# VectorE's duties planned gap by gap between the evictions of a shared PSUM bank

## The reference

```python
x = x + attn(layernorm(x))
x = x + ffn(layernorm(x))
# attn
q, k, v = split(h @ qkv_w.T)                    # 16 heads of 16
q_weights = exp(|q - centers|^2 * inv_var)      # 16 splats per head; k_weights alike
logits = einsum('bihs,bjhs,hs->bijh', q_weights, k_weights, amplitudes) / temp
out = softmax(logits, over j) @ v, then @ out_w.T
# ffn
xr, xk = mu * h + (1 - mu) * h_prev             # h_prev: the token before
out = sigmoid(xr @ W_r.T) * (relu(xk @ W_k.T)**2 @ W_v.T)
```

## Time and profile before

| | |
|---|---|
| median of 3 runs | 2163.5 us (2162.55 to 2164.25) |
| the profiled execution | 2162.01 us |
| its span, first to last instruction | 2160.2 us |
| mean granted TensorE clock | 0.998 |
| instructions | 52461 |

### The profile page before, as it was taken

One profiled execution on the slowest core, in us unless ns is written; L12 is line 12 of the kernel. 1 busy time (PEld: TensorE's weight loads), 2 busy tenths in 40 slices (PEclk: granted clock), 3 DMA queues, 4 the chain that ended last, 5 costly groups with the idle time before them and its releaser, 6 DMA issues.

```text
span 2160.2 us, 52461 instructions
## 1 busy us (share of the span) xinstructions
PE 2129.8 (99%) x22996; PEld 975.8 (45%) x22996; DVE 742.1 (34%) x1684; ACT 2013.2 (93%) x2190; POOL 386.5 (18%) x486
## 2 busy tenths in 40 slices
PE   7999999999999999999999999999999999999999
PEld 5444444444444444444444444444444444444445
DVE  5324433233432432433323334324323223323225
ACT  3899999999999999999999999999999999999995
POOL 0244243333100142022101203320310000000000
PEclk9999999999999999999999999999999999999999
DMA  6554445353221334316131332523252141311111
GB/s 179 141 147 121 123 125 147 107 154 112 67 68 51 94 109 109 97 41 174 27 91 28 112 94 72 138 60 99 61 144 53 41 90 41 61 30 48 33 41 44
DMA packets 176232, 193.06 MB, mean 89 GB/s; under 512 B 88529, under 2 KB 108369, under 8 KB 175985
## 3 DMA queue, kind: packets, MB, share of 16 engines
q1 hardware_dynamic: 166720, 174.69, 29.3%
q0 software_dynamic: 7168, 14.69, 2.7%
q10 hardware_dynamic: 2096, 0.14, 0.1%
HBM read 98.90 MB, written 75.81 MB: 81 GB/s over the span
## 4 chain that ended last, share of the span: by engine, by line
PE 90%; ACT 7%; DVE 2%; issue 1%; DMA 0%; DVEq 0%
PE ps_pv L889 40%; PE ps_scores L870 27%; PE ps_step L917 17%; ACT probs L1214 6%; PE ps_step L938 2%; PE ps_scores L902 1%; PE ps_step L896 1%; PE ps_scores L907 1%; ACT weight L1278 0%; PE ps_scores L912 0%; PE ps_scores L911 0%; DMA x_prep<-x 0%; DVE weight L1478 0%; DVE ffn_stats L1381 0%; DVE h_ffn L1395 0%
## 5 line engine op out<-in xcount | busy, mean ns | idle before, releaser
L1214 ACT ACTIVATE probs<-ps_scores 128x1024 f32<-128x1024 f32 x2048 | 1941.1, 1030 | 82.7 <-PE ps_scores L870 56.4
L889 PE MATMUL ps_pv<-probs,vals 128*32 128x512 f32 (+5 forms) x10104 | 1079.8, 520 | 0.0
L870 PE MATMUL ps_scores<-q_aug,k_aug 49*128 49x512 f32 x4096 | 706.2, 442 | 8.1 <-ACT probs L1214 5.9
L870 PEld LDWEIGHTS ps_scores<-q_aug,k_aug 49*128 49x128 f32 x4096 | 331.2, 184 | 617.2 <-ACT probs L1214 563.6
L889 PEld LDWEIGHTS ps_pv<-probs,vals 128*32 128x32 f32 x10104 | 349.4, 139 | 201.1 <-issue 118.2
L1336 POOL DMA_DIRECT2D packed<-qk x224 | 113.5, 512 | 871.9 <-DVE qk L1501 850.2
L1341 POOL TENSOR_TENSOR packed<-qk 32x512 f32<-32x512 f32 x224 | 238.2, 1064 | 16.9
L1346 POOL TENSOR_TENSOR k_act<-k_act 128x512 f32<-128x512 f32 x28 | 29.5, 1054 | 817.8 <-DVE k_act L1504 817.8
L1567 DVE COPY o_raw<-ps_pv 128x512 f32<-128x512 f32 x63 | 43.6, 691 | 247.3 <-PE ps_pv L889 246.6
L1501 DVE COPY qk<-ps_step 128x512 f32<-128x512 f32 x56 | 38.7, 690 | 223.9 <-PE ps_step L917 223.9
L1478 DVE TENSOR_SCALAR weight<-ps_step,cen_sq 128x512 f32<-128x512 f32 x57 | 42.8, 750 | 198.0 <-PE ps_step L938 197.1
(11 more groups left out here) (207 smaller groups left out, 1126.6 us busy)
## 6 DMA issues: line engine op xcount, KB each, us to landing
k_aug<-k_parts SPq DMA_DIRECT2D x128, 192.0 KB, 5.0
q_aug<-q_parts SPq DMA_DIRECT2D x128, 192.0 KB
k_parts<-parts SPq DMA_DIRECT2D x32, 512.0 KB, 3.3
q_parts<-parts SPq DMA_DIRECT2D x32, 512.0 KB, 4.7
packed<-qk POOLq DMA_DIRECT2D x224, 64.0 KB, 2.2
x_ffn<-x SPq DMA_DIRECT2D x18, 512.0 KB, 4.8
k_parts<-parts SPq DMA_DIRECT2D x32, 256.0 KB, 4.0
q_parts<-parts SPq DMA_DIRECT2D x32, 256.0 KB, 5.3
```

The lines of the kernel that those rows point to most:

```text
L870: mm = pe.matmul(ps_scores[:, g % RING, e, :], k_aug[rows, s % 2, pair, kt * P:(kt + 1) * P], q_aug[rows, u % 2, pair, :], start=True, sto ...
L889: mm = pe.matmul(ps_pv[32 * c:32 * c + 32, at], vals[:, s % 2, kt, :, c], probs[:, tick % PROB_SLOTS, c, at], start=(kt == 0), stop=(kt == ...
L1214: act.activation(probs[:, tick % PROB_SLOTS, 2 * pair:2 * pair + 2, :], ps_scores[:, g % RING, :, :], ACT.Exp).then_inc(probs_ready, 1)
```

## The change

The places of the duties are no longer fixed ticks but come from a planner, `pace_duties`. Each duty has an earliest tick (the one it had before, for most), a due tick, a tick by which it is needed at a reduction of maxima, and a price (a gap has 12). The planner goes through the gaps in order. In a gap it adds up the prices of the evictions and the take, and then puts in the ready duty with the earliest due tick, as long as the sum stays within the gaps up to the next one (`GAP_WORK * (gap + 2)`); a duty whose due tick is passed or is at most one tick ahead goes in regardless. Within a tick the order is now spread, invert, scaling, ffn layernorm, mix, done, norm, statistics, split.

`norm_tick` moves from 5 to 9 ticks ahead of k0, and with it the earliest ticks of statistics and norm, and SP's ticks for the store and the load of the norm rows. `x_tick` gives the same ticks as before. TensorE's, ScalarE's and GpSimd's programs stay as they are, and so do VectorE's evictions and takes.

The core of the diff:

```diff
 def norm_tick(task):
-    return max(begin(task, "k0") - 5, 1)
+    return max(begin(task, "k0") - 9, 1)
...
+DUTIES = {
+    "spread": [(KT * (u + 1) + 1, KT * (u + 1) + 3, KT * (u + 1) + 4, 3, u) for u in range(UNITS - 1)],
+    "invert": [(KT * (u + 1) + 2, KT * (u + 1) + 4, KT * (u + 1) + 4, 4, u) for u in range(UNITS - 1)],
+    "scale": [(KT * (u + 1) + 3, KT * (u + 1) + 5, KT * (u + 1) + 4, 3, u) for u in range(UNITS - 1)],
+    "ffn_ln": [(tick, begun(task, "turn0") - 4 + part, begun(task, "turn0"), (8, 5, 5, 6)[part], (task, part))
+               for tick, found in FFN_LN_AT.items() for task, part in found],
...
+    "stats": [(tick, tick + 3, norm_tick(task) - 8, (8, 5, 6)[part], (task, part)) for tick, found in STATS_AT.items() for task, part in found],
...
+}
+GAP_WORK = 12
+URGENT = 1
+EVICT_WORK = 3
+OVER = 1
...
+def pace_duties():
...
+    for gap in range(2 * EVENT_TICKS // 3):
+        tick, end_of_next = name_of(gap), GAP_WORK * (gap + 2)
+        now = max(now, GAP_WORK * (gap + 1)) + EVICT_WORK * ((tick in evicts) + (gap in takes))
+        held = name_of(gap + 1) in evicts
+        until = name_of(gap + 1) if name_of(gap + 1) in MAX_AT else 0
+        while True:
+            forced = [duty for duty in waiting if duty[2] <= until and duty[0] < until]
+            ready = forced or [duty for duty in waiting if duty[0] <= tick + 1 - gap % 2]
+            if not ready:
+                break
+            duty = min(ready, key=lambda duty: (duty[1], duty[0], duty[3]))
+            _, due, _, kind, which, work = duty
+            if not forced and due > tick + URGENT and now + (work - OVER if held else 0) > end_of_next:
+                break
+            paced[DUTY_ORDER[kind]].setdefault(tick, []).append(which)
...
-                for u in LEAVE_AT.get(tick, ()):
+                for u in DUTY_AT["spread"].get(tick, ()):
                     spread(u)
```

More of the change, by code:

```diff
@@ L391, with begun @@
 DONE_AT = beside((end(task, "v1") + 1, task) for task in FFNS if task != LAST_BUT)
+def begun(task, name):
+    return begin(task, name) if (task, name) in SPAN else EVENT_TICKS
+DUTIES = {
[4 more added lines that the diff above has]
+               for tick, found in FFN_LN_AT.items() for task, part in found],
+    "mix": [(tick, begun(task, "r0") - 2 + part if part < 2 else begun(task, "k0") - 4 + part,
+             begun(task, "r0") if part < 2 else begun(task, "k0"), 5, (task, part))
+            for tick, found in MIX_AT.items() for task, part in found],
+    "done": [(tick, tick + 6, tick + 1, 5, task) for tick, found in DONE_AT.items() for task in found],
+    "norm": [(tick, begun(task, "k0") - 2 + half, norm_tick(task) + 2, 6, (task, half)) for tick, found in NORM_AT.items() for task, half in found],
+    "stats": [(tick, tick + 3, norm_tick(task) - 8, (8, 5, 6)[part], (task, part)) for tick, found in STATS_AT.items() for task, part in found],
+    "split": [(tick, tick + 3 - side, split_tick(task, half, 1) + 2, (5, 6)[side], (task, half, side)) for tick, found in SPLIT_AT.items() for task, half, side in found],
+}
@@ new lines, with gap_of_values @@
+DUTY_ORDER = list(DUTIES)
+GAP_WORK = 12
+URGENT = 1
+EVICT_WORK = 3
+OVER = 1
+def gap_of_values(tick):
+    return 2 * ((tick + 2) // 3) + int(tick % 3 == 0)
+def pace_duties():
+    waiting = sorted((tick, due, need, DUTY_ORDER.index(kind), which, work) for kind, found in DUTIES.items()
+                     for tick, due, need, work, which in found)
+    evicts = {tick for tick, found in EVICT_AT.items() if any(task[0] != "ffn" or name not in ("r0", "r1") for task, name in found)}
+    takes = {gap_of_values(KT * (u + 1) - 1) for u in range(UNITS - 1)}
+    paced = {kind: {} for kind in DUTY_ORDER}
+    now = 0
+    for gap in range(2 * EVENT_TICKS // 3):
[13 more added lines that the diff above has]
+            paced[DUTY_ORDER[kind]].setdefault(tick, []).append(which)
+            now += work
+            waiting.remove(duty)
+    assert not waiting, waiting[:3]
+    return paced
@@ L394, in load @@
+DUTY_AT = pace_duties()
 def load(gap):
@@ L1688, in _ @@
                     take(tick // KT)
-                for u in LEAVE_AT.get(tick, ()):
+                for u in DUTY_AT["spread"].get(tick, ()):
                     spread(u)
-                for u in LEAVE_AT.get(tick - 1, ()):
+                for u in DUTY_AT["invert"].get(tick, ()):
                     invert(u)
@@ L1694, in _ @@
                     replicate(u, slice(0, CHUNK)).then_inc(den_inverted, 1)
-                for u in LEAVE_AT.get(tick - LEFT_TICKS + 1, ()):
+                for u in DUTY_AT["scale"].get(tick, ()):
                     v.wait_ge(den_inverted, INVERT_STEPS * (u + 1))
                     v.tensor_tensor(o_raw[:, u % 2, :], o_raw[:, u % 2, :], den_all[:, :], ALU.mult).then_inc(scaled, 1)
[L1698 to L1708, removed]
+                for task, part in DUTY_AT["ffn_ln"].get(tick, ()):
                     n = FFN_NO[task]
@@ L1712, in _ @@
                     layernorm("ffn", n, x_ffn[:, n % 2, :, :], h_ffn, ffn_ln, part)
-                for task, half, side in SPLIT_AT.get(tick, ()):
+                for task, part in DUTY_AT["mix"].get(tick, ()):
+                    mix(task, part)
+                for task in DUTY_AT["done"].get(tick, ()):
+                    n = FFN_NO[task]
+                    v.wait_ge(step_free, STEP_NO[task, "v1"] + 1)
+                    finish(n, slice(0, TT)).then_inc(finished, 1)
+                for task, half in DUTY_AT["norm"].get(tick, ()):
+                    normed_columns(task, half)
+                for task, part in DUTY_AT["stats"].get(tick, ()):
+                    statistics(task, part)
+                for task, half, side in DUTY_AT["split"].get(tick, ()):
                     late_split(task, half, side)
```

## The result

| kernel | median us (lowest to highest, runs) | profiled execution: time, span |
|---|---|---|
| before | 2162.65 (2161.99 to 2164.25, 20) | 2162.01, 2160.2 |
| after | 2165.77 (2163.22 to 2168.42, 20) | 2167.36, 2165.5 |

The ratio is 1.0014, with a 95% interval from 1.0007 to 1.0020: slower by 0.14%, which lies inside the 0.2% that was called no change ahead. The forecast, 2169.8, was 4.0 us too high. Of these, 0.9 are the median of before, which these 20 runs put at 2162.65; the other 3.2 are the change, which was forecast at +6.3 and is +3.1. The kernel after also varies more, over 5.2 us where the kernel before varies over 2.3.

The account below looks back on a forecast made before the run. TensorE and ScalarE were taken as each other's bound, VectorE able to give back under 15.6 us. Terms +3.3, +3.4 and -0.4 made +6.3 us on the 2163.5 median: 2169.8, range 2163 to 2174.5.

Parts of the forecast that it names:

- Place one: At (prep 1,1) statistics wait for x, delaying dist_k0: 4.6 us, clock 1.7, less 3.0 at k1; net +3.3 (-0.8 to +6.6).
- Place two: At turn0 of (ffn 0,3), (1,0), (2,0), (3,1), the layernorm's part 3 comes later: +3.4 us in sum.
- the forecast's other side: At the four turn0, ScalarE might hold 0.4 us at each, leaving 1.8 us of the 3.4.
- The clock's price for the first of the four: At turn0 of (ffn 0,3), if TensorE's clock falls at 916 us, 1.7 us on top, making the four 5.1.
- Small gains: At turn0, dist_k1 and v1, evictions no longer late: -0.4 us for the three together, bounds 0 and 1.2.
- All else: Other duties, SP's other waits and norm rows shift slightly; slack covers them, so no cost.
- The forecast's own case: Whole kernel slower by +4.3 to +9 us, around +6.3; chance 0.60.
- losses absorbed: Rival: SP, clock or ScalarE's ring hides part; +1.5 to +2.3 us, within 0.2%, 2165 us; chance 0.25.
- The planner doing what it says: Rival: faster by 4.7 us, 2158.8, if x lands before 216.0 us, so is issued by 209.6; chance 0.06.
- GpSimd's work lengthening a duty: Rival: duties behind q or k evictions run 0.8 us longer; five add 4 us, 2174 us; chance 0.06.
- three signs of being wrong: x lands by 216 us, ScalarE shows no idle stretch behind the waits, or new late evictions stand elsewhere.
- these eleven: Eleven evictions start over 0.2 us late behind the attention bank's take at the same tick boundary; said to stay.

Follow-up runs that it names:

- the layernorm edit: Kernel after, with the due ticks of the four ffn layernorm parts three ticks earlier: 2160.13 us, ratio 0.9990 to before.
- eviction ahead of take: Kernel after with x loaded 30 ticks ahead, layernorm parts due three ticks earlier, and at twelve ticks VectorE's product copy put before the take: 2154.13 us.
- both edits: Kernel after with loads of x 30 instead of 24 ticks ahead of k0 and layernorm parts due three ticks earlier: 2158.17 us, ratio 0.9978 to before.
- the scaling earlier: Kernel after with the scaling of unit 3 one tick earlier, ahead of the first query take's eviction: 2163.53 us, ratio 1.0002 to before.
- the second with the old constant: Kernel after with norm_tick back to 5 ticks ahead of k0, planner kept, run and traced a second time: 2163.24 us.
- x earlier: Kernel after with loads of x and its columns 30 instead of 24 ticks ahead of k0: 2163.45 us, ratio 1.0003 to before.

## Why the prediction came out as it did

**Place one: the mechanism was right in each link, the size was nearer to that of the two traces with the late landing.** Issue of x "near 216" was 215.2 to 216.1, dist_q0's load was forecast to be free at 225.0 and was at 225.01 in the profiled execution, its wait forecast at 4.6 was 4.42. The step that was off is that x "lands 6.4 us later", taken from one row. In the four traces it is 5.3 twice and 7.2 or 7.3 twice, and with 5.3 the net of place one is 1.61 + 0.14 - 3.35 = -1.6, a small gain, against +1.9 with 7.3 and +3.3 forecast. The bounds given, -0.8 to +6.6, hold +1.9 and miss -1.6. The forecast looked for its lower bound in SP being in time, and not in a load that lands early.

**The terms of place one.** Where the clock falls, the loss is 5.26 us against the 6.3 of the forecast. Its parts can be told by setting the traces with 2.43 us of waiting and a full clock beside those with 4.42 and half: the former cost 1.75, so of a wait the usual 0.27 and 0.4 more don't count (that ScalarE's ring holds the 0.4 is argued, not shown); the clock is 1.5 where 1.7 was forecast. 4.42 - 0.27 - 0.4 + 1.5 = 5.25. The forecast had left out both subtractions (0.4 as a bound at turn0 alone), and at k1 it took 3.0 where 3.36 came back. Together that is 1.4 us of the 3.2 between forecast and measured change. If the early landings, worth 3.5 us, come in about half of the executions, as in two of four traces, they make the other 1.8; this is an estimate from four traces.

**Place two was right:** 3.4 forecast, 3.76 measured at once and 3.4 for good, each of the four within 0.12 us. At first ScalarE hides none of it, one for one as argued from the row at 919.50; three exponentials later it has back 0.14, 0.14 and 0.08 us of three of them, where the forecast's other side allowed 0.4 at each. The clock's price for the first of the four, kept as a bound, is paid in some executions and not in others.

**Small gains** were -0.4 and are -0.34. **"All else" at nothing** held: no further step over 0.3 us, except the early stretch at half clock, which lasts 3.41 us in three of the thirteen traces (before, the layernorm edit, and eviction ahead of take) and 6.83 in the ten others. The kernel before was traced once, so whether the change has a part in that is open. In the profiled execution it cost 0.8 us, a term that the forecast doesn't have.

**The rivals.** The forecast's own case, +4.3 to +9 with a chance of 0.60, did not come true by its time, though the time lies inside the range. The case that did is the one given 0.25, losses absorbed (within 0.2%), with its size of +1.5 to +2.3 just under the measured +3.1. By its reasons it is half true: at place one a load that lands early hides part, at turn0 0.36 us of 3.76 come back and the rest counts. The planner doing what it says is what both edits together show, 4.7 us under before, the size worked out for it. Its condition was put too hard, though: x issued at 212.81, not by 209.6, was enough for place one to cost nothing, since a wait that ends before dist_q0 wants the bank at 220.4 is free, and the statistics need not end before dist_k0 is ready. Of GpSimd's work lengthening a duty there is no step in the account, and the mean of a scaling fell from 742 to 728 ns, that of the last part of the weights' split from 871 to 782: the duties got shorter on the whole, with no gain in the account to go with it. None of the three signs of being wrong came: x landed after 216, ScalarE idled behind both waits, and no new late eviction stands elsewhere with a step over 0.3 us.

**"The order of eviction and take is not touched, so these eleven stay"** was right for the change, and is where much was left: 4.0 us by the medians, some 3 of them seen at these places, beside 4.7 for all that the planner with both edits wins over before.

## What to carry to other kernels

A duty that waits for a transfer must not be planned by the time that it takes alone: in an in-order queue its price is the landing of the transfer, and it belongs behind the next eviction, or its load ahead of every queue that the plan slows down. Where a step ends on a transfer, take two or three landing times from the trace and work the sum out for each: landings 2 us apart made the sign of place one here. And a part that is due "one tick before its reader" was late here wherever an eviction, a spread or an invert came to stand ahead of it; here two constants turned a loss of 3.1 us into a gain of 4.7, with the planner left as it was.

## What the runs showed of the hardware

The load of x, 512 KB in one transfer, took 5.3, 5.3, 7.2 and 7.3 us to land in four executions of one kernel, issued within 1.0 us of the same time; with the layernorm edit it took 5.9, with the scaling earlier 5.1 and before the change 6.4, so there are more than two values. What decides it is not shown: the transfers issued around it are the same, and the DMA share over 217 to 223 us is 1.00 to 1.05 in all four. The Trainium skill's page "DMA: Bandwidth & Descriptors", section "Latency and other measured facts", gives HBM's access as 0.2 us on average and 2 us at high load. The difference of 2.0 us is of that size, but the DMA share is the same with either landing and no run here varies the load on memory, so that this is the cause is not shown.

TensorE's granted clock after a wait is not settled by the wait. Behind 4.42 us it fell to 0.5 (1.2 GHz) in both traces that have that wait, behind 2.96 us in the one trace of the layernorm edit, behind 2.43 and 2.44 us in neither, and behind 2.05 or 2.06 us at the first turn0 in one trace and not in seven others (four of the kernel after, the second with the old constant, and those with x earlier and with the scaling earlier). Before the change it fell behind the 2.30 us of the earlier trace rows. The two falls that could be set beside the same place without one cost 1.5 and 1.6 us. What decides whether it falls is not shown. A wait of 2 to 3 us thus has a price that comes in some executions and not in others. That price, the landing of x and the early stretch at half clock are what the traces show of the spread of the times: the two kernels in which dist_q0's load waits for x vary by 5.2 and 5.5 us, before and the others by 1.3 to 3.1.
